# An attention and MLP layer in fp32: the place of one P V product, ScalarE's order of copies at two changes of weights, and the low halves of three weights in pieces

## The chip, the cores and the metric

One core of one Trainium2 chip. The metric is the device time of one execution of the whole program, in microseconds (us); lower is better. Three executions of the kernel before took 2776.44, 2777.89 and 2778.57 us. The names of the engines in the profile: PE (TensorE, matrix products), PEld (its weight loads), DVE (VectorE), ACT (ScalarE), POOL (GpSimd) and SP (SyncE, which issues the DMAs).

## The reference

Sixteen batches, each a 512 x 512 query x and a 512 x 512 context, go through one layer with 16 heads of 32:

```python
q = _layer_norm(query, ln1_g, ln1_b)
qh, kh, vh = q @ wq + bq, context @ wk + bk, context @ wv + bv
scores = einsum('bqhd,bkhd->bhqk', qh, kh) / sqrt(32)
scores = where(k <= q, scores, -inf)
o = einsum('bhqk,bkhd->bqhd', softmax(scores), vh)
x = query + o @ wo + bo
h = _layer_norm(x, ln2_g, ln2_b)
out = x + gelu(h @ w1 + b1) @ w2 + b2
```

w1 is 512 x 2048 and w2 is 2048 x 512. All is fp32.

## The kernel before

Dense products are made from two halves of each operand, a high half rounded to the short form fp32r and a low half, the rest: three matmuls (high x high, high x low, low x high) give one product. As a rule ScalarE writes a high half (a COPY or CAST) and VectorE the low half (a subtraction that waits for it).

**Preparation** (up to about 37 us). The four weights of attention are loaded; ScalarE writes their high halves and VectorE, in `weight_low` (L720), the low halves of wk, wv and wo, each with one instruction on 128 x 2048 elements. GpSimd at the same time splits the context of batch 0 into its halves, in `context` (L958): a CAST at L962 and a subtraction at L964 for each of four blocks. K's first product on TensorE (job K0) takes a block kt when `c_done` says so (L472).

**Stage A, attention** (to about 1424 us). Per batch there are 4 groups of 4 heads, and per group 12 steps; a step handles one tile of scores. Tiles k = 0 to 3 of a group (pair 0) hold the first two blocks of 128 queries of one head, tiles 4 to 11 (pair 1) one block each. Tile n = 12 g + k goes round like this: `score` (L500) on TensorE in step n; `mask_and_max` (L659) on VectorE; `exponential` (L852) on ScalarE; in groups 0 and 1 `scale` on GpSimd (L979); three steps later `p_transpose` (L515) on TensorE, into bank_t[n % 2]; in step n + 4 `move_tile` (L599) from that bank to pT, on ScalarE where `ACT_MOVES` names the tile and else on VectorE. When all tiles of a pair of a group are moved, `pv` (L528) multiplies them with V: pair 0 of group g in step 9 of that group, pair 1 in step 5 of the next. The buffers are narrow: `score` n waits for the mask of tile n - 2 (two banks), `p_transpose` n for the move of tile n - 2 (two banks), and a move of the next group's tile of a pair for that pair's `pv`.

Every engine runs the steps in the order of its own `body`. TensorE's (L576) is, in one step,

```python
score(it, n)
for job, i, j in steps:
    dense_step(it, job, g, i, j)
if k == PV1_AT and not (it.first and g == 0):
    pv(it, g - 1, 1)
if k == PV0_AT and not it.tail:
    pv(it, g, 0)
if n >= LAG and not it.tail or n < LAG and not it.first:
    p_transpose(it, n - LAG)
```

The dense jobs of table `BESIDE` fill the steps: in group 2, K3 in steps 2 and 3, V0b in 4 to 6, V1b in 7 to 9 and X0 to X3 (the transposes of the next batch's normalised x) in 7 to 10. For these VectorE computes the statistics and the normalisation (L627 to L640) in group 2's steps 1 and 4 to 7, ScalarE and VectorE the halves of the transposed x (`x_high` L825, `x_low` L643), and ScalarE copies V out (`v_copy`, L841) after the move of its step and ahead of the exponential. The first batch has no output products (jobs O and R), the last one no X jobs.

**Stage B, the MLP** (from about 1424 us) runs over the batches twice, once per half of the hidden units (phases 0 and 1). Its products use Strassen's scheme with 7 partial products. At the first batch of each phase (`first`) the halves of w2, and at the entry of part of w1, are still to be made: `w1_high` (L1689) and `w2_high` (L1707) on ScalarE, `w1_parts` and `w2_parts` (L1427, L1467) on VectorE, with sums (T1 to T4, S1 to S4) on VectorE between them. ScalarE's `body` (L1766) also copies the products P1, P5 and U2 of each half d out of TensorE's banks (`copy`, L1722): step (d, 3) of TensorE waits for P1's copy, (d, 4) for P5's and (d, 5) for U2's (L1319 to L1325). `a_high` (L1741) and VectorE's `a_low` make the halves of the activations for the second layer's products, `layer2` (L1338).

## Time and profile before

| what | value |
|---|---|
| median of 3 executions | 2777.89 us |
| the profiled execution's own time | 2778.07 us |
| its span, first to last instruction | 2776.2 us |
| mean granted clock of TensorE | 0.995 |
| PE, DVE, ACT, POOL busy | 98%, 74%, 60%, 32% of the span |
| one batch of attention (from one L687 of its group 2 to the next, 345.61 to 431.94) | 86.33 us |

The times in the rows count from the span's start. A row of the timeline has the start, the duration, the engine, the line, the operation with output and input, and how many instructions it merges; in brackets stands how long the engine had been idle, and who released it. Instructions of one engine overlap a little at their ends.

### The profile page before, as it was taken

Reading aid. Unit: us, or ns where it says so; the run is one execution under the profiler, and the core shown is the slowest. Engines: PE = TensorE matmul, PEld = TensorE weight load, DVE = VectorE, ACT = ScalarE, POOL = GpSimd, SP = SyncE. Lnnn points to the kernel's source line nnn. Section 1 sums busy time; section 2 is a strip of 40 time slices with the busy share of each in tenths; the row PEclk is TensorE's granted clock in tenths of the full one; section 3 lists DMA queues with packets and bytes.
Section 4 is the critical chain, followed back from the end, with each engine's and each line's share of the span. In section 5 each row is a group of like instructions: output and inputs, shape, how many; then the busy total and the mean of one; then the engine's idle time right before and its main releaser. Section 6 shows DMA issues by size and latency. Waiting matters only on the chain.

```text
span 2776.2 us, 67352 instructions
## 1 busy us (share of the span) xinstructions
PE 2730.1 (98%) x21928; PEld 2489.3 (90%) x21928; DVE 2041.0 (74%) x5205; ACT 1654.4 (60%) x4017; POOL 893.4 (32%) x842
## 2 busy tenths in 40 slices
PE   7999999999999999999979999999998999999999
PEld 6888888888888888888869999999998999999999
DVE  6777777777777777777698787787788566566556
ACT  5766667666676666766665656656556445444444
POOL 6657566575765656656510000000000000000000
PEclk9999999999999999999999999999999999999999
DMA  5233333333333323333243533534435433343342
GB/s 186 104 126 132 118 118 118 129 131 111 121 117 129 133 106 125 121 130 124 100 163 130 196 146 148 196 135 160 191 126 197 160 145 141 129 166 136 122 157 99
DMA packets 153084, 383.58 MB, mean 138 GB/s; under 512 B 13440, under 2 KB 17536, under 8 KB 144768
## 3 DMA queue, kind: packets, MB, share of 16 engines
q1 hardware_dynamic: 152960, 382.28, 37.1%
q14 instruction: 90, 0.74, 0.1%
q8 instruction: 34, 0.56, 0.1%
HBM read 172.51 MB, written 109.05 MB: 101 GB/s over the span
## 4 chain that ended last, share of the span: by engine, by line
PE 94%; DVE 2%; issue 2%; POOL 1%; ACT 1%; DMA 0%; SPq 0%; DVEq 0%; POOLq 0%; ACTq 0%
PE bank_d L495 19%; PE bank_t L525 11%; PE bank_s L1299 7%; PE bank_d L490 7%; PE bank_s L1300 6%; PE bank_s L1301 6%; PE bank_s L510 6%; PE bank_v L548 5%; PE bank_d L1299 5%; PE bank_d L1301 5%; PE bank_d L1300 5%; PE bank_v L1299 2%; PE bank_v L1300 2%; PE bank_v L1301 2%; PE bank_t L1299 1%
## 5 line engine op out<-in xcount | busy, mean ns | idle before, releaser
L862 ACT ACTIVATE sm<-sm,mins 128x128 f32<-128x128 f32 (+3 forms) x1024 | 572.0, 559 | 439.2 <-DVE mins L670 434.6
L989 POOL TENSOR_SCALAR sm<-sm,recips 128x128 f32<-128x128 f32 (+3 forms) x512 | 549.8, 1084 | 235.9 <-DVE recips L682 234.1
L670 DVE CUSTOM_DVE_ANT_0 sm<-bank_s,mask 128x128 f32<-128x128 f32 (+3 forms) x1024 | 474.3, 484 | 66.8 <-PE bank_s L510 64.0
L615 DVE COPY pT<-bank_t 128x384 f32<-128x384 f32 (+1 forms) x544 | 306.8, 564 | 210.6 <-PE bank_t L525 208.5
L1299 PE MATMUL bank_s<-w_hi,a_hi 128*128 128x256 f32 x1536 | 435.6, 284 | 2.1 <-DVE a_lo L1425 2.1
L1300 PE MATMUL bank_s<-w_lo,a_hi 128*128 128x256 f32 x1536 | 435.0, 283 | 0.0
L1301 PE MATMUL bank_s<-w_hi,a_lo 128*128 128x256 f32 x1536 | 434.9, 283 | 0.0
L525 PE MATMUL bank_t<-ident,sm 128*128 128x128 f32 x2560 | 412.8, 275 | 10.5 <-POOL sm L989 3.4
L525 PEld LDWEIGHTS bank_t<-ident,sm 128*128 128x128 f32 x2560 | 306.6, 140 | 92.3 <-issue 32.7
L1299 PE MATMUL bank_d<-b_hi,w_hi 128*128 128x256 f32 x1280 | 369.8, 289 | 14.0 <-ACT g L1726 7.7
L1301 PE MATMUL bank_d<-b_hi,w_lo 128*128 128x256 f32 x1280 | 364.3, 285 | 0.0
L1300 PE MATMUL bank_d<-b_lo,w_hi 128*128 128x256 f32 x1280 | 364.1, 284 | 0.0
L510 PE MATMUL bank_s<-stack 128*128 128x128 f32 (+3 forms) x1024 | 351.6, 384 | 0.0
L1299 PEld LDWEIGHTS bank_s<-w_hi,a_hi 128*128 128x128 f32 x1536 | 295.4, 192 | 3.1 <-DVE xr L1552 2.0
L1300 PEld LDWEIGHTS bank_s<-w_lo,a_hi 128*128 128x128 f32 x1536 | 295.3, 192 | 0.0
L1301 PEld LDWEIGHTS bank_s<-w_hi,a_lo 128*128 128x128 f32 x1536 | 295.2, 192 | 0.0
L1299 PEld LDWEIGHTS bank_d<-b_hi,w_hi 128*128 128x128 f32 x1280 | 247.5, 193 | 15.9 <-DVE w_lo L1425 14.2
L1506 DVE TENSOR_TENSOR g<-bank_d,g 128x512 f32<-128x512 f32 x160 | 110.4, 690 | 189.0 <-PE bank_d L1301 188.2
L1300 PEld LDWEIGHTS bank_d<-b_lo,w_hi 128*128 128x128 f32 x1280 | 247.8, 194 | 0.0
L1301 PEld LDWEIGHTS bank_d<-b_hi,w_lo 128*128 128x128 f32 x1280 | 247.5, 193 | 0.0
L1737 ACT ACTIVATE g<-g,vecb 128x256 f32<-128x256 f32 x384 | 174.7, 502 | 110.5 <-DVE g L1506 108.3
L1751 ACT CAST a_hi<-g 128x512 fp32r<-128x512 f32 x256 | 158.8, 621 | 113.6 <-PE bank_s L1301 110.9
(161 smaller groups left out, 6550.2 us busy)
## 6 DMA issues: line engine op xcount, KB each, us to landing
stack<-st_hi SPq DMA_DIRECT2D x256, 256.0 KB, 2.4
stack<-st_lo SPq DMA_DIRECT2D x128, 256.0 KB, 2.4
xr<-x_scratch SPq DMA_DIRECT2D x64, 512.0 KB, 4.2
b_scratch<-b_hi SPq DMA_DIRECT2D x16, 1792.0 KB, 9.1
b_scratch<-b_lo SPq DMA_DIRECT2D x16, 1792.0 KB, 12.8
b_hi<-b_scratch SPq DMA_DIRECT2D x16, 1792.0 KB, 7.3
b_lo<-b_scratch SPq DMA_DIRECT2D x16, 1792.0 KB, 11.2
xt<-in_x SPq DMA_DIRECT2D x64, 256.0 KB, 2.7
```

The lines of the kernel that those rows point to most:

```text
L490: mm = pe.matmul(out, left[part // 2][:, kt, cols], right[part % 2][:, kt, rows], start=(n == 0), stop=(n >= 18), skip_group_check=True)
L495: mm = pe.matmul(out, left[part // 2][:, kt, cols], right[part % 2][:, kt, rows], start=(at == 0), stop=(at == 11))
L510: mm = pe.matmul(bank_s[n % BANKS_S][:, off:off + w], stack[:, g % 2, 0, r, P * qt:P * qt + P], stack[:, g % 2, 1, r, 0:w], start=True, st ...
L525: mm = pe.transpose(bank_t[n % 2][:, P * c:P * c + P], sm[:, n % SLOTS_S, P * c:P * c + P], ident[:])
L615: copy(out, src).then_inc(moved[n % 2], 1)
L670: op = V.tensor_tensor_reduce(sm[:, n % SLOTS_S, off:off + w], bank_s[n % BANKS_S][:, off:off + w], mask[:, 512 - w:512], 1.0, 0.0, ALU.ad ...
L862: op = A.activation(row, row, ACT.Exp, bias=mins[:, g % 2, c:c + 1], scale=-1.0, accum_out=sums[:, g % 2, c:c + 1])
L989: op = G_.tensor_scalar(out=row, in0=row, scalar1=recips[:, g % 2, c:c + 1], scalar2=None, op0=ALU.mult)
L1299: pe.matmul(o, lh, rh, start=opens, stop=False, skip_group_check=True)
L1300: pe.matmul(o, lh, rl, start=False, stop=False, skip_group_check=True)
L1301: return pe.matmul(o, ll, rh, start=False, stop=True, skip_group_check=True)
L1737: op = A.activation(to, bank_x[d][:, C * m:C * m + C] if name == "C21" else to, ACT.Gelu, bias=vec[:, f:f + 1], scale=1.0)
```

## The change

1. In group 2, `pv` of group 1 runs in step 3, pair 0 and pair 1 one after the other, instead of pair 0 in group 1's step 9 and pair 1 in group 2's step 5. The other groups keep their places.
2. Of group 1's tiles ScalarE moves k = 3, 5 and 9 instead of 5, 9 and 11.
3. `weight_low` issues four subtractions of 128 x 512 instead of one of 128 x 2048; only the last one signals.
4. At the entry of stage B ScalarE makes S1 and S3 of w1 after the copy of P1 instead of before it.
5. At the first batch of each phase ScalarE copies P1, P5 and U2 of the half d = 1 ahead of most of the high halves of w2 that stood before them, and the activation high half (1, 0) comes after U2.

```diff
--- before.py
+++ after.py
@@ -41,7 +41,7 @@
     return 1, (k - 4) // 2, (2 + (k - 4) % 2,)
 
 
-ACT_MOVES = [(5, 9, 11), (5, 9, 11), (3, 5, 7, 9, 11), (5, 9, 11)]
+ACT_MOVES = [(5, 9, 11), (3, 5, 9), (3, 5, 7, 9, 11), (5, 9, 11)]
 
 
 def act_moves(n):
@@ -102,7 +102,7 @@
     TAIL = [("R", {5: 4}), ("O0", {7: 9, 8: 3}), ("O1", {7: 6, 9: 6}), ("O2", {10: 12}), ("O3", {11: 12})]
 
 
-    R_AT, PV1_AT, PV0_AT, O_PROD_AT, O_HIGH_AT, O_HIGH_LATE = 4, 5, 9, 6, 7, 11
+    R_AT, PV1_AT, PV0_AT, PV_AT, O_PROD_AT, O_HIGH_AT, O_HIGH_LATE = 4, 5, 9, 3, 6, 7, 11
 
     FEED_X_AT = 6
     STATS_AT, NORMALISE_AT = ((1, 8), (1, 11), (2, 1), (2, 4)), ((2, 5), (2, 6), (2, 6), (2, 7))
@@ -585,9 +585,13 @@
                         score(it, n)
                     for job, i, j in steps:
                         dense_step(it, job, g, i, j)
-                    if k == PV1_AT and not (it.first and g == 0):
+
+                    if k == PV_AT and g == 2:
+                        pv(it, g - 1, 0)
                         pv(it, g - 1, 1)
-                    if k == PV0_AT and not it.tail:
+                    if k == PV1_AT and g != 2 and not (it.first and g == 0):
+                        pv(it, g - 1, 1)
+                    if k == PV0_AT and g != 1 and not it.tail:
                         pv(it, g, 0)
                     if n >= LAG and not it.tail or n < LAG and not it.first:
                         p_transpose(it, n - LAG)
@@ -719,9 +723,10 @@
 
             def weight_low(i, done):
                 dve.wait_ge(w_hi_done, KT + i)
-                V.tensor_tensor(w_lo[i][:].rearrange("p t n -> p (t n)"), raw[i],
-                                w_hi[i][:].rearrange("p t n -> p (t n)").bitcast(F32),
-                                ALU.subtract).then_inc(done, 1)
+                for kt in range(KT):
+                    op = V.tensor_tensor(w_lo[i][:, kt, :], raw[i][:, D * kt:D * kt + D],
+                                         w_hi[i][:, kt, :].bitcast(F32), ALU.subtract)
+                op.then_inc(done, 1)
 
             for t in range(QT):
                 x_low(pro, f"X{t}", 0, 0)
@@ -942,8 +947,6 @@
                     if it.tail and n == 10:
                         feed_h_high("T4")
                         feed_w1_high(1, 1, ["A11", "A22", "A12"])
-                    if it.tail and n == 11:
-                        feed_w1_high(1, 1, ["S1", "S3"])
 
             over_batches(act, body)
             act.wait_ge(dense, tail_it.done("O3", 0))
@@ -1769,7 +1772,7 @@
             U = 4 * ph
             copy(c, 0, "P1")
             if first:
-                w1_high(U + 1, 1, ["S2"])
+                w1_high(U + 1, 1, ["S1", "S3", "S2"] if ph == 0 else ["S2"])
             copy(c, 0, "P5")
             if first:
                 w1_high(U + 1, 1, ["S4"])
@@ -1780,24 +1783,34 @@
             if first:
                 w2_high(U + 2, 0, ["B11", "B21", "B22"])
             activate(c, ph, 0, "C22")
+            copy(c, 1, "P1")
             if first:
-                w2_high(U + 2, 0, ["T1", "T3", "T2", "T4"])
-            copy(c, 1, "P1")
-            activate(c, ph, 0, "C21")
-            a_high(c, 1, 0)
-            if first:
-                w2_high(U + 3, 1, ["B11", "B21", "B22"])
-            copy(c, 1, "P5")
-            if norm:
-                x_high(c + 1, 0, x_bank(0))
-            if switch:
-                w1_high(4, 0, ["A11", "A22"])
-            activate(c, ph, 1, "C11")
-            if first:
-                w2_high(U + 3, 1, ["T1", "T3"])
-            if norm:
-                x_high(c + 1, 1, x_bank(1))
-            copy(c, 1, "U2")
+
+                w2_high(U + 2, 0, ["T1", "T3"])
+                activate(c, ph, 0, "C21")
+                copy(c, 1, "P5")
+                if norm:
+                    x_high(c + 1, 0, x_bank(0))
+                w2_high(U + 2, 0, ["T2", "T4"])
+                copy(c, 1, "U2")
+                a_high(c, 1, 0)
+                w2_high(U + 3, 1, ["B11", "B21", "B22", "T1"])
+                activate(c, ph, 1, "C11")
+                w2_high(U + 3, 1, ["T3"])
+                if norm:
+                    x_high(c + 1, 1, x_bank(1))
+            else:
+                activate(c, ph, 0, "C21")
+                a_high(c, 1, 0)
+                copy(c, 1, "P5")
+                if norm:
+                    x_high(c + 1, 0, x_bank(0))
+                if switch:
+                    w1_high(4, 0, ["A11", "A22"])
+                activate(c, ph, 1, "C11")
+                if norm:
+                    x_high(c + 1, 1, x_bank(1))
+                copy(c, 1, "U2")
             a_high(c, 0, 1)
             if norm:
                 x_high(c + 1, 2, x_bank(2))
```

The order of instructions at two places, as the program issues it. First TensorE at the start of group 2, from the end of step 3 (the last matmuls of K3) into step 4; L525 are the transposes of a tile, L510 scores, L490 the first matmuls of V0b, L548 is P V. Before:

```order
L495 MATMUL bank_d<-cT_hi,wk_lo 128x512
L525 MATMUL bank_t<-ident,sm 128x128 x3
L510 MATMUL bank_s<-stack 128x384
L490 MATMUL bank_d<-wv_hi,cT_hi 128x256
L490 MATMUL bank_d<-wv_lo,cT_hi 128x256
```

and with the change:

```order
L495 MATMUL bank_d<-cT_hi,wk_lo 128x512
L548 MATMUL bank_v<-pT,v_sb 32x256 x4
L548 MATMUL bank_v<-pT,v_sb 32x128 x4
L548 MATMUL bank_v<-pT,v_sb 32x256 x12
L548 MATMUL bank_v<-pT,v_sb 32x128 x4
L525 MATMUL bank_t<-ident,sm 128x128 x3
L510 MATMUL bank_s<-stack 128x384
L490 MATMUL bank_d<-wv_hi,cT_hi 128x256
```

Both blocks of P V now stand between K3 and the transposes of group 2's first tile (tile 24). In group 1, where pair 0 stood between the output product and the transposes of tile 18, it is gone.

Then ScalarE at the first batch of stage B, from the activation C22 of half 0 (L1737, with the change L1740) to the activations of half 1; L1705 (L1708) are high halves of w2, L1726 (L1729) the copies P1, P5 and U2 and L1751 (L1754) the activations' high halves, L1686 (L1689) the next batch's x. Before:

```order
L1737 ACTIVATE g<-g,vecb 128x256 x2
L1705 CAST w_hi<-s_sums 128x512 x2
L1705 CAST w_hi<-spare 128x512 x2
L1726 COPY g<-bank_d 128x2x256
L1737 ACTIVATE g<-bank_v,vecb 128x256 x2
L1751 CAST a_hi<-s_sums 128x512
L1705 CAST w_hi<-xr 128x512 x3
L1726 COPY g<-bank_d 128x2x256
L1686 ACTIVATE hT<-bank_t,vecb 128x512
L1737 ACTIVATE g<-g,vecb 128x256 x2
```

and with the change:

```order
L1740 ACTIVATE g<-g,vecb 128x256 x2
L1729 COPY g<-bank_d 128x2x256
L1708 CAST w_hi<-s_sums 128x512 x2
L1740 ACTIVATE g<-bank_v,vecb 128x256 x2
L1729 COPY g<-bank_d 128x2x256
L1689 ACTIVATE hT<-bank_t,vecb 128x512
L1708 CAST w_hi<-spare 128x512 x2
L1729 COPY g<-bank_d 128x2x256
L1754 CAST a_hi<-s_sums 128x512
L1708 CAST w_hi<-xr 128x512 x4
```

The first copy of a bank (P1) now comes before four high halves of w2 instead of after them, the second before the last two of these, and the third right behind them.

## Rows read from the trace of the kernel before

**Rows 1.** The page: the chain that ended last, by engine.

```profile
PE 94%; DVE 2%; issue 2%; POOL 1%; ACT 1%; DMA 0%; SPq 0%; DVEq 0%; POOLq 0%; ACTq 0%
```

**Rows 2.** Busy us of PE, PEld, DVE, ACT, POOL by stretch (stretch, its length, then busy).

```profile
340.00:354.00 14.00, 14.00 (x143) 12.45 (x142) 12.29 (x33) 9.27 (x23) 5.62 (x6) 1.00 0.20 76
1424.00:1471.00 47.00, 36.06 (x242) 34.38 (x241) 40.52 (x72) 32.20 (x61) 1.39 (x1) 0.82 0.33 128
2124.00:2153.00 29.00, 20.87 (x151) 19.91 (x150) 25.39 (x42) 18.73 (x38) 0.00 (x0) 0.88 0.32 111
```

**Rows 3.** Timeline of PE, batch 3, group 1 (start, us, engine, line, work).

```profile
318.37 1.72 PE L548 MATMUL bank_v<-pT,v_sb 128*32 128x256 f32 x32
...
327.18 0.39 PE L495 MATMUL bank_d<-wo_hi,oT_hi 128*128 128x512 f32 x1
327.40 0.40 PE L495 MATMUL bank_d<-wo_lo,oT_hi 128*128 128x512 f32 x1
327.73 0.86 PE L548 MATMUL bank_v<-pT,v_sb 128*32 128x256 f32 x16
328.52 0.55 PE L525 MATMUL bank_t<-ident,sm 128*128 128x128 f32 x3
328.82 0.42 PE L510 MATMUL bank_s<-stack 128*128 128x384 f32 x1
```

**Rows 4.** Timeline of PE, batch 3, group 2 and the start of 3.

```profile
339.37 0.49 PE L525 MATMUL bank_t<-ident,sm 128*128 128x128 f32 x3
...
354.07 0.49 PE L525 MATMUL bank_t<-ident,sm 128*128 128x128 f32 x3
354.32 0.47 PE L510 MATMUL bank_s<-stack 128*128 128x128 f32 x2
```

**Rows 5.** Timeline of DVE in the same stretch.

```profile
339.99 0.56 DVE L615 COPY pT<-bank_t 128x384 f32<-128x384 f32 x1 [0.97 <-PE bank_t L525]
...
344.67 0.56 DVE L615 COPY pT<-bank_t 128x384 f32<-128x384 f32 x1 [0.30 <-PE bank_t L525]
...
349.34 0.55 DVE L670 CUSTOM_DVE_ANT_0 sm<-bank_s,mask 128x384 f32<-128x384 f32 x1
...
352.57 0.69 DVE L648 TENSOR_TENSOR xnT_lo<-bank_d,xnT_hi 128x512 fp32r<-128x512 f32 x1 [0.76 <-ACT xnT_hi L828]
353.18 0.55 DVE L615 COPY pT<-bank_t 128x384 f32<-128x384 f32 x1
353.64 0.55 DVE L670 CUSTOM_DVE_ANT_0 sm<-bank_s,mask 128x384 f32<-128x384 f32 x1
```

**Rows 6.** Timeline of ACT in the same stretch.

```profile
349.89 0.59 ACT L828 CAST xnT_hi<-bank_d 128x512 fp32r<-128x512 f32 x1 [0.72 <-PE bank_d L438]
350.38 0.62 ACT L862 ACTIVATE sm<-sm,mins 128x384 f32<-128x384 f32 x1
...
351.94 0.60 ACT L828 CAST xnT_hi<-bank_d 128x512 fp32r<-128x512 f32 x1
```

**Rows 7.** Timeline of PE, batch 0, group 1.

```profile
70.80 0.66 PE L525 MATMUL bank_t<-ident,sm 128*128 128x128 f32 x4 [0.48 <-POOL sm L989]
```

**Rows 8.** Timelines of POOL, DVE and PE in the preparation.

```profile
14.47 1.59 POOL L962 CAST cT_hi<-c_raw 128x512 fp32r<-128x512 f32 x1 [2.15 <-DVE xt L640]
...
23.69 2.67 POOL L962 CAST cT_hi<-c_raw 128x512 fp32r<-128x512 f32 x1
...
14.19 1.41 DVE L708 SCALAR_TENSOR_TENSOR wq_lo<-pT,wq_scale,wq_hi 128x512 fp32r<-128x512 f32 x2
...
23.39 2.50 DVE L722 TENSOR_TENSOR wv_lo<-sm,wv_hi 128x2048 fp32r<-128x2048 f32 x1
...
27.75 0.50 PE L495 MATMUL bank_d<-cT_hi,wk_hi 128*128 128x512 f32 x1 [3.00 <-POOL cT_lo L964]
```

**Rows 9.** Timelines of PE at the entry and of DVE at the change of halves.

```profile
1443.57 0.66 PE L1291 MATMUL bank_t<-ident,xn 128*128 128x128 f32 x4 [1.93 <-DVE xn L1421]
...
2139.50 1.29 DVE L1425 TENSOR_TENSOR w_lo<-hT,w_hi 128x512 fp32r<-128x512 f32 x2 [1.48 <-ACT w_hi L1705]
```

## The prediction

> **What bounds the kernel now.** I read the page first: TensorE is busy 98% of the span, by its part on the engines, and makes 94% of the chain that ended last [rows 1]. So time goes only where TensorE loses an instruction's time, or gets a new wait. Then the busy time by stretch: in group 2 of a batch (steps 4 to 11) TensorE is busy 14.00 of 14.00 us, but VectorE 12.29 of them as well, with 1.7 us to spare; at the change of stages TensorE is busy 36.06 of 47.00 and VectorE 40.52, at the change of halves 20.87 of 29.00 and 25.39 [rows 2]. There TensorE waits, and VectorE is what it waits for in the long run. Last the timelines of one batch, read for who is how late; inner batches repeat with a period of 86.33 us.
>
> **Part 1, P V of group 1 in one block: the saving.** In group 1 the block of pair 0 starts 0.33 us after the last output matmul (327.40), and the transposes follow 0.79 later, at 328.52; output matmuls are 0.22 to 0.23 apart. The scores behind follow the transposes by 0.30 instead of 0.25 [rows 3, 4]. So the block costs 1.12 - 0.23 + 0.05 = 0.94 us. The block of pair 1 (x32 in the row, 1.72 us) is 0.86 longer than that of pair 0 (x16) for 512 more columns, 1.68 ns each [rows 3]. Pair 0's 384 columns thus need 0.645 us of work; the other 0.29 us is for getting into the small tiles and out of them. In one block with pair 1 it is paid once: TensorE saves 0.29 us a batch, 4.7 us over 16.
>
> **Part 1, what it makes late.** The block now stands ahead of the transposes of tile 24. TensorE gets there 0.94 us earlier than before, so the block starts at 339.37 - 0.94 + 0.10, and takes 0.65 + 1.65: the transposes go at 340.83 instead of 339.37 [rows 4], 1.46 later, though what follows V0b is 0.29 earlier. VectorE's copy of that tile, which waited for them at 339.99 [rows 5], is as late. VectorE has no gap from there to its wait at 344.67, 0.30 us long, 0.40 with the 0.1 by which two instructions may overlap. So from 344.67 on VectorE is 1.46 - 0.40 = 1.06 us late, where TensorE is 0.29 early. The two engines stood still in step with each other before; now VectorE runs behind.
>
> Up to step 8 the buffers hold it. I followed scores and transposes one by one: the mask of tile 29 is done some 0.2 us before its scores' bank is wanted, the normalised x of X0 0.1 us before. Then ScalarE, whose exponentials wait for the masks, runs without the gap of 0.72 us that it had at 349.89 [rows 6]. It takes the delay on: the mask of tile 32 at 349.34 [rows 5] becomes 350.40, the exponential behind it 350.98 instead of 350.38, and the CAST of X2 (third in line) 352.54 instead of 351.94 [rows 6]. VectorE's low half follows 0.63 behind that CAST (352.57 before), then the copy of tile 30 at 353.78 instead of 353.18, done at 354.33 [rows 5]. The transposes of tile 32 need its bank. They went at 354.07 [rows 4], and would go at 353.78: they **wait to 354.35, 0.56 us**. The next scores, due 0.25 later, need the mask of tile 34, which moves from 353.64 to 354.24 and is done at 354.87: another 0.30. Sum 0.86 lost, 0.29 saved: **0.57 us slower per batch**. VectorE is level again with TensorE two steps later, so nothing goes on into group 3. Fourteen inner batches: +8.0 us.
>
> Batch 0: its group 1 has no output products, and TensorE waits there for GpSimd's scaling just behind the place the block is taken from (0.48 us at 70.80 [rows 7]), so the 0.94 us earlier is mostly not had: 0.57 + 0.94 = +1.5. The last batch has no X jobs and no statistics: VectorE catches up, -0.3. **Part 1 in all: +9.2 us.** Bounds per inner batch: -0.29 (nothing binds) and +1.2 (0.86 lost and, of 1.06, the rest too, with nothing saved).
>
> **Part 2, ScalarE's moves.** A COPY of some 0.6 us goes from VectorE to ScalarE at step 19 of a batch and back at step 27. At step 27 VectorE stood idle 0.97 us before 339.99 [rows 5], which covers it, and the block waits for this copy no longer than for K3 to end. Nothing gained, nothing lost. Without that cover the block itself would start up to 0.6 late.
>
> **Part 3, the low halves in pieces.** Only the last piece signals, so what can change is GpSimd. Its CAST at 14.47 took 1.59 us and the one at 23.69 took 2.67, ending both times 0.47 us after VectorE's subtractions of two operands in SBUF [rows 8]. TensorE waited 3.00 us for the block behind the second. In the first case VectorE ran two pieces one behind the other (x2, 14.19 to 15.60), and GpSimd did not get in between them. I take that row: no entry at a seam. Then pieces only add their seams. The nearest bound is 1.41 us for two pieces of 512, so at most 2.8 for four against 2.5 [rows 8]; less here, where a plain subtraction of 512 lets the next start after 0.61 (352.57 to 353.18 [rows 5]). I take 0.2 for each of wk and wv, both on the way to GpSimd's last block: **+0.4 us**. The other bound is the whole wait gone, -3.0. wo's pieces end before the first mask is due.
>
> The Trainium skill, "SBUF — State Buffer", section "Who interferes with whom", says that VectorE with two SBUF inputs and GpSimd reading SBUF exclude each other for a whole instruction, and that the second to issue is blocked until the first finishes. By that rule each seam would let GpSimd in, after 0.6 us instead of 2.3, and the sum would have -3.0 in place of +0.4. The row at 14.47 speaks against it.
>
> **Parts 4 and 5, the order of copies.** At the entry P1's copy comes 2 us earlier, but TensorE then meets its wait for the normalised x at 1443.57 [rows 9], which hangs on VectorE's unbroken work ahead of it: nothing is left of it. After it, TensorE's steps (1, 3) to (1, 5) no longer wait for ScalarE's copies, which are most of the 8.1 us that it is idle at the change of halves [rows 2]. It runs up to 8 us ahead, and then waits in `layer2` for VectorE's a_low (0, 1), and again for (1, 1) and (2, 0). VectorE had only 3.6 us without work in those 29 us, and 6.5 of 47 at the entry [rows 2]. The longest of these gaps, 1.48 us before the low half of T1 at 2139.50 [rows 9], closes, since T1's high half now comes ahead of an activation; about 0.5 opens elsewhere, as T1 and T2 of w2's first part come behind a copy of 0.6. **-1.0 at the change of halves, -0.9 at the entry**, which has the same queue and the next batch's x in it. Bounds: 0, and the gaps whole, -3.6 and -6.5.
>
> **Sum** against the profiled execution's 2778.07 us (span 2776.2): 9.2 + 0.4 - 1.9 = +7.7, so 2785.8. The median of the runs is 0.2 lower than that execution: **2785.6 us**.
>
> **The rivals.**
> 1. *The seams let GpSimd in*, part 1 as above. TensorE's K0 ends 3.0 us earlier. For it: GpSimd waits there for nothing else, its loads having landed. Against: the row at 14.47. 2785.6 - 3.4 = 2782.2 us. By the skill's rule this is the case. Chance 0.25.
> 2. *VectorE's lateness does not reach TensorE* (the other side, faster). The place is the transposes of tile 32. Before, tile 30's copy ended at 353.73, 0.34 us ahead of them [rows 4, 5]; if VectorE and ScalarE make good all but 0.05 us of the delay by then, 0.29 us a batch is kept: -4.7 + 0.4 - 1.9, 2771.7 us, and 2768.3 with rival 1. For it: 1.7 us of slack in 14 [rows 2]. Against: the gaps are mostly waits for ScalarE, which is late itself. Chance 0.22.
> 3. *The lateness costs at V's and X's banks too*: X3 takes V1b's bank, which ScalarE's copy frees; by my count it is free 0.04 us in time. If ScalarE is 0.5 later there, each batch loses 0.5 more: +7, 2793 us. Chance 0.08.
>
> My forecast has 0.45; its own range is 2783 to 2789 (0.2 us either way per batch, and half of the last part). **Range** 2769 to 2789: it leaves out rival 3 and the tail of rival 2. A measurement of this kernel tells 0.2% (5.6 us) from no change: faster is below 2772.3, slower above 2783.4. Faster: rival 2 but for its edge, 0.2. Same: rival 1 and edges, 0.29. Slower: 0.51.
>
> **What would show it.** Part 1: blocks of x48 rows on L548 in group 2, one batch 86.9 us instead of 86.33, and TensorE waiting about 0.5 us for VectorE's pT before the transposes at the end of group 2, in each inner batch; VectorE idle near 3 us ahead of tile 24's copy. If those waits are missing, rival 2 holds. Part 3: GpSimd's CASTs beside wk's and wv's low halves still above 2 us; at 0.6 to 1.2, rival 1. Parts 4 and 5: the waits for ScalarE's g gone, one wait of some 5 us for a_lo in their place. I am wrong if the period stays below 86.33, or if the two changes give over 3 us each.

## The result and the profile after

The changed kernel takes 2784.1 us in the median of 11 runs (2782.58 to 2785.43), the kernel before, run beside it, 2776.36 (11 runs, 2774.25 to 2778.57). The ratio is 1.0028, with a 95% interval of 1.0021 to 1.0036: slower, by 7.7 us. The time and its cause in attention came as forecast. Two smaller terms had the wrong sign, and the errors nearly cancelled.

The profiled execution of the changed kernel has a span of 2783.0 us, 6.8 more than the one before. To see where that lies I take marks that are in both programs: VectorE's COPYs out of the P V bank, two in each batch (one in group 1, one in group 2), and its sums out of bank_t in stage B. In the timeline of VectorE before (start, us, engine, line, work) they are these; the first row is the first COPY of batch 0, the second and third are the second COPYs of batches 3 and 4, the fourth is the last COPY of attention:

```profile
65.95 0.67 DVE L687 COPY rT<-bank_v 128x512 f32<-128x512 f32 x1
...
345.61 0.69 DVE L687 COPY rT<-bank_v 128x512 f32<-128x512 f32 x1
...
431.94 0.68 DVE L687 COPY rT<-bank_v 128x512 f32<-128x512 f32 x1
...
1381.84 0.68 DVE L687 COPY rT<-bank_v 128x512 f32<-128x512 f32 x1
...
1483.54 0.70 DVE L1552 TENSOR_TENSOR xr<-bank_t,xr 128x512 f32<-128x512 f32 x1
...
2115.19 0.70 DVE L1552 TENSOR_TENSOR xr<-bank_t,xr 128x512 f32<-128x512 f32 x1
...
2163.54 0.68 DVE L1552 TENSOR_TENSOR xr<-bank_t,xr 128x512 f32<-128x512 f32 x1
```

And after:

```profile
63.09 0.67 DVE L691 COPY rT<-bank_v 128x512 f32<-128x512 f32 x1
...
346.35 0.68 DVE L691 COPY rT<-bank_v 128x512 f32<-128x512 f32 x1
...
433.31 0.68 DVE L691 COPY rT<-bank_v 128x512 f32<-128x512 f32 x1
...
1389.38 0.69 DVE L691 COPY rT<-bank_v 128x512 f32<-128x512 f32 x1
...
1491.52 0.68 DVE L1555 TENSOR_TENSOR xr<-bank_t,xr 128x512 f32<-128x512 f32 x1
...
2123.17 0.68 DVE L1555 TENSOR_TENSOR xr<-bank_t,xr 128x512 f32<-128x512 f32 x1
...
2170.39 0.68 DVE L1555 TENSOR_TENSOR xr<-bank_t,xr 128x512 f32<-128x512 f32 x1
```

The differences between neighbours give the ledger of the 6.8 us:

| stretch | before, us | after, us | difference | forecast |
|---|---|---|---|---|
| start to the first P V copy (the preparation) | 65.95 | 63.09 | -2.86 | +0.4 |
| first to last P V copy (attention) | 1315.89 | 1326.29 | +10.40 | +9.2 |
| to the first sum out of bank_t (entry of stage B) | 101.70 | 102.14 | +0.44 | -0.9 |
| across the change of halves | 48.35 | 47.22 | -1.13 | -1.0 |

From batch 1 on, the P V copies of neighbouring batches stand 86.32 us apart before, in most batches, and 86.96 after. The ledger compares one execution of each kernel.

**Attention.** In the timeline of TensorE the place of the block and the place of the wait look like this (start, us, engine, line, work, and in brackets the idle time and what ended it):

```profile
338.14 2.37 PE L548 MATMUL bank_v<-pT,v_sb 128*32 128x256 f32 x48
340.44 0.55 PE L525 MATMUL bank_t<-ident,sm 128*128 128x128 f32 x3
...
352.94 0.60 PE L525 MATMUL bank_t<-ident,sm 128*128 128x128 f32 x4
353.30 0.48 PE L510 MATMUL bank_s<-stack 128*128 128x512 f32 x1
354.15 0.52 PE L525 MATMUL bank_t<-ident,sm 128*128 128x128 f32 x3 [0.37 <-DVE pT L619]
354.53 0.50 PE L510 MATMUL bank_s<-stack 128*128 128x128 f32 x2
```

The block is one of x48. The transposes of tile 32 answer to those at 354.07 [rows 4], and they wait for VectorE's copy of pT. The bracket gives 0.37 us, but they start 0.85 us behind the scores ahead of them (353.30), where the kernel before has 0.32, counted from this row of its timeline of TensorE:

```profile
353.75 0.48 PE L510 MATMUL bank_s<-stack 128*128 128x512 f32 x1
```

So 0.53 us are lost at this place, and another 0.13 at the scores behind (0.38 us behind their transposes instead of 0.25). Over the whole program this kind of wait went from 2.5 us in 4 places to 8.0 us in 19 (the waits of TensorE, after: line waited for, us in total, times, longest):

```profile
PE bank_t L525 <- DVE pT L619: 8.0, 19, 1.3
```

VectorE itself, in the same stretch, has a hole behind the block and then none until a wait for ScalarE at 352.85:

```profile
341.12 0.56 DVE L619 COPY pT<-bank_t 128x384 f32<-128x384 f32 x1 [3.11 <-PE bank_t L525]
...
345.41 0.55 DVE L619 COPY pT<-bank_t 128x384 f32<-128x384 f32 x1
...
352.85 0.69 DVE L652 TENSOR_TENSOR xnT_lo<-bank_d,xnT_hi 128x512 fp32r<-128x512 f32 x1 [1.01 <-ACT xnT_hi L833]
353.46 0.55 DVE L619 COPY pT<-bank_t 128x384 f32<-128x384 f32 x1
```

The COPY at 345.41 is the one that had waited 0.30 us at 344.67 [rows 5]: the gap is gone, as the forecast had it.

**Preparation.** GpSimd's CASTs of the context answer to those at 14.47 and 23.69 [rows 8]:

```profile
14.39 0.94 POOL L965 CAST cT_hi<-c_raw 128x512 fp32r<-128x512 f32 x1 [2.15 <-DVE xt L644]
...
19.88 0.81 POOL L965 CAST cT_hi<-c_raw 128x512 fp32r<-128x512 f32 x1 [0.95 <-DMA c_raw<-in_ctxT]
...
22.30 1.07 POOL L965 CAST cT_hi<-c_raw 128x512 fp32r<-128x512 f32 x1
```

The fourth CAST, 2.67 us before, now takes 1.07, and it runs beside wk's pieces instead of wv's low half. The price is on VectorE and shows in TensorE's wait, now for wk's low half instead of for GpSimd (first VectorE, then TensorE):

```profile
18.92 3.97 DVE L727 TENSOR_TENSOR wk_lo<-pT,wk_hi 128x512 fp32r<-128x512 f32 x4
...
22.95 0.50 PE L495 MATMUL bank_d<-cT_hi,wk_hi 128*128 128x512 f32 x1 [1.78 <-DVE wk_lo L727]
```

**Stage B.** At the entry and at the change of halves TensorE waits once for a long time for VectorE's a_low (timeline of TensorE):

```profile
1441.21 0.55 PE L1302 MATMUL bank_d<-b_hi,w_hi 128*128 128x256 f32 x1 [2.84 <-ACT g L1729]
...
1452.67 0.66 PE L1294 MATMUL bank_t<-ident,xn 128*128 128x128 f32 x4 [1.42 <-DVE xn L1424]
...
1468.26 0.55 PE L1302 MATMUL bank_s<-w_hi,a_hi 128*128 128x256 f32 x1 [6.14 <-DVE a_lo L1428]
...
2149.00 0.56 PE L1302 MATMUL bank_s<-w_hi,a_hi 128*128 128x256 f32 x1 [5.13 <-DVE a_lo L1428]
```

The transposes at 1452.67 answer to 1443.57 [rows 9]: 9.1 us later. The program is 7.5 us late at the start of this stretch, so 1.6 are lost between.

### The profile page after: what moved, and what is told of

It reads as the page before. It is cut to its first block, busy times and chain, and to the rows that moved or that the text cites. A ratio compares the mean times of both kernels' runs of the same rounds, so it can differ in the third digit from the quotient of the medians.

```text
span 2783.0 us, 67361 instructions
## 1 busy us (share of the span) xinstructions
PE 2731.0 (98%) x21928; PEld 2488.2 (89%) x21928; DVE 2039.8 (73%) x5214; ACT 1652.3 (59%) x4017; POOL 890.5 (32%) x842
## 4 chain that ended last, share of the span: by engine, by line
PE 48%; DVE 2%; issue 1%; ACT 1%; POOL 0%; DMA 0%; DVEq 0%; ACTq 0%; POOLq 0%
PE bank_s L1302 6%; PE bank_s L1303 6%; PE bank_s L1304 6%; PE bank_d L1302 5%; PE bank_d L1304 5%; PE bank_d L1303 5%; PE bank_v L1302 2%; PE bank_v L1303 2%; PE bank_v L1304 2%; PE bank_d L495 1%; PE bank_t L1302 1%; PE bank_t L1304 1%; PE bank_t L1303 1%; PE bank_t L525 1%; PE bank_t L1294 1%
## 5 line engine op out<-in xcount | busy, mean ns | idle before, releaser
L525 PE MATMUL bank_t<-ident,sm 128*128 128x128 f32 x2560 | 412.5, 275 | 16.8 <-DVE pT L619 8.0
L525 PEld LDWEIGHTS bank_t<-ident,sm 128*128 128x128 f32 x2560 | 305.9, 140 | 98.7 <-issue 29.7
L510 PE MATMUL bank_s<-stack 128*128 128x128 f32 (+3 forms) x1024 | 351.8, 384 | 0.0
L1740 ACT ACTIVATE g<-g,vecb 128x256 f32<-128x256 f32 x384 | 174.6, 502 | 108.6 <-DVE g L1509 106.6
L1754 ACT CAST a_hi<-g 128x512 fp32r<-128x512 f32 x256 | 158.7, 621 | 113.6 <-PE bank_s L1304 110.8
```

Source lines behind the costliest of these rows:

```text
L510: mm = pe.matmul(bank_s[n % BANKS_S][:, off:off + w], stack[:, g % 2, 0, r, P * qt:P * qt + P], stack[:, g % 2, 1, r, 0:w], start=True, st ...
L525: mm = pe.transpose(bank_t[n % 2][:, P * c:P * c + P], sm[:, n % SLOTS_S, P * c:P * c + P], ident[:])
L1740: op = A.activation(to, bank_x[d][:, C * m:C * m + C] if name == "C21" else to, ACT.Gelu, bias=vec[:, f:f + 1], scale=1.0)
L1754: A.copy(a_part(a_hi, k, h), a_source(k, h)).then_inc(a_hi_ok, 1)
```

## The experiments

Each kernel is told as a change of the kernel before or of the changed one, with its five readings in the table at the end of this section.

**pieces** has part 3 alone.

> The kernel before with nothing but the low halves of wk, wv and wo in four pieces each. Theory: the whole 2.9 us by which the first copy out of the P V bank came earlier in the changed kernel (65.95 to 63.09 us) comes from this part, since GpSimd gets into the seams between pieces; the run is then 2.9 us under the kernel before (ratio 0.9990), with that copy near 63.1. Rival, what my prediction held: GpSimd gets no seam and the pieces cost 0.4 us; the 2.9 came from elsewhere (another state of the entry), and the copy is near 66.3.

**pv_moves** has parts 1 and 2 alone, **pv_only** part 1 without the new list of moves:

```
-ACT_MOVES = [(5, 9, 11), (3, 5, 9), (3, 5, 7, 9, 11), (5, 9, 11)]
+ACT_MOVES = [(5, 9, 11), (5, 9, 11), (3, 5, 7, 9, 11), (5, 9, 11)]
```

> The kernel before with nothing but both P V blocks of group 1 in step 3 of group 2 and the list of ScalarE's copies of group 1. Theory: it carries all of the loss of attention, 10.4 us (ratio 1.0037), 0.63 us in each middle batch (period 86.33 to 86.96 us). Rival: part of the loss of a batch is made by the other parts (through SBUF state or code loading), and this run stays under 8 us.

> As pv_moves, but with ScalarE's copies of pT in group 1 at tiles 5, 9 and 11 as before. Theory: the list of copies is worth nothing beside the block (prediction: 0), so this run is within 0.1 us per batch of pv_moves, 9 to 12 us over the kernel before. Rival: the block is what costs and the new list gives part of it back, since it takes the copy of tile 23 off ScalarE where the x copies queue; then this run is 2 us or more slower than pv_moves.

**after_stats** is the changed kernel with one number changed:

```
-    STATS_AT, NORMALISE_AT = ((1, 8), (1, 11), (2, 1), (2, 4)), ...
+    STATS_AT, NORMALISE_AT = ((1, 8), (1, 11), (2, 1), (2, 3)), ...
```

> The changed kernel with the fourth row statistic of the next batch (statistics of tile 3, the aggregates and the sum with epsilon, 1.2 us of VectorE's time) one step earlier, in step 3 of group 2, where VectorE idles 3.1 us behind the P V block. Theory: TensorE's loss of a batch is VectorE's lateness behind that hole (waits of 0.37 us for the copy of pT at tile 32 and more for scores), so filling the hole takes it away: the period falls from 86.96 to about 86.0 (the saving of one entry into tile mode then stands alone, 0.3 under the period of before), the time to about 2770. Rival: the loss is in TensorE itself (a block of two P V lengths with nothing beside it, or tile mode entered at a worse place); then the period stays at 86.9 and the time at 2784.

Measured, beside a kernel before of 2777.47 us (21 runs): pieces 2774.68 us, ratio 0.9994 (0.9985 to 1.0003); pv_moves 2788.22, 1.0035 (1.0021 to 1.0049); pv_only 2785.56, 1.0036 (1.0022 to 1.0049); after_stats 2769.38, **0.9974 (0.9965 to 0.9983)**, faster than both kernels.

The block alone carries the loss in attention: the period is 86.97 us in pv_moves and in pv_only, so the list of moves is worth nothing there. (pv_only is 8.1 us over the kernel before, a little under the 9 to 12 expected; with 5 runs each the medians of the two kernels don't tell them apart.) The statistic decides between the two theories on part 1. VectorE now does it in the hole (timeline of VectorE, after_stats):

```profile
334.68 0.69 DVE L631 BATCH_NORM_STATS2 stats<-xt 128x6 f32<-128x512 f32 x1
335.28 0.41 DVE L637 BATCH_NORM_AGGREGATE mv<-stats 128x2 f32<-128x6 f32 x4
...
337.87 0.56 DVE L619 COPY pT<-bank_t 128x384 f32<-128x384 f32 x1 [1.97 <-PE bank_t L525]
```

and TensorE goes through the end of the group without a wait (timeline of TensorE, after_stats; the third and fourth row answer to 354.15 and 354.53 above):

```profile
349.46 0.60 PE L525 MATMUL bank_t<-ident,sm 128*128 128x128 f32 x4
349.81 0.48 PE L510 MATMUL bank_s<-stack 128*128 128x512 f32 x1
350.13 0.49 PE L525 MATMUL bank_t<-ident,sm 128*128 128x128 f32 x3
350.38 0.47 PE L510 MATMUL bank_s<-stack 128*128 128x128 f32 x2
```

The period is 86.03, 0.29 under the 86.32 of before: the saving that I had read out of the two block lengths. (The runs show it for one block less; that it is the way into and out of the small tiles is the reading, and no run separates it.) The loss of a batch was VectorE's lateness, and it was 86.96 - 86.03 = 0.93 us.

A reading of pieces against the others was not what I expected. The first P V copy is at 63.90 us, 2.05 earlier than before, but in pv_only, which has no pieces at all, it is at 62.27. So the early start isn't the pieces' alone. That made the next experiments compare the preparation too.

**before_stats** is the control: the same number changed in the kernel before.

> Control for after_stats: the kernel before with the same statistic one step earlier and nothing else. Theory: in the kernel before VectorE has no hole in that step and TensorE does not wait for it at tile 32, so moving 1.2 us of VectorE's work is worth nothing: period 86.32 us as before, time within 1 us of the kernel before. Rival: the statistic's place is what limits either kernel and the gain has nothing to do with the P V block; then the period falls by 0.3 us or more here too, to 2772 or less.

**entry_b** has part 4 alone, **halves** part 5 alone, and **after_stats_s13** is after_stats with part 4 taken back:

```
+                    if it.tail and n == 11:
+                        feed_w1_high(1, 1, ["S1", "S3"])
...
-                w1_high(U + 1, 1, ["S1", "S3", "S2"] if ph == 0 else ["S2"])
+                w1_high(U + 1, 1, ["S2"])
```

> The kernel before with nothing but the copies of S1 and S3 of the second half moved behind the copy of P1 at the entry of stage B. Stretch measured: from the last copy out of the P V bank of attention's last group to the first sum out of bank_t, 101.70 us before. Theory: the order of ScalarE gives 0.9 us (100.8), as in the changed kernel with the statistics moved (100.76), and the 102.14 of the changed kernel has 1.4 us of TensorE at half clock on top, which does not belong to the edit. Rival: the edit itself brings the half clock (TensorE waits 2.8 us for a copy just there) and costs 0.4 (102.1). The time is within 1 us of the kernel before by either; the stretch decides.

> The kernel before with nothing but the copies P1, P5 and U2 of half 1 ahead of the high halves of w2, in the first batch of each phase. Stretch measured: between the sums out of bank_t on either side of the change of halves, 48.35 us before, 47.22 in the changed kernel. Theory: the gain of 1.1 us there is this part's alone: 47.2, and nothing elsewhere (first stretch 101.7 by this part, and more only if its edit in the first batch of phase 0 acts there). Rival: it needs the other edit of ScalarE's order; then 48.3. Time about 2776, 1 us under the kernel before.

> The changed kernel with the statistic moved as in after_stats, and S1 and S3 back where they stood before, in attention's last step. Theory: part 4 is worth 0.9 us, so this run is 0.9 us slower than after_stats (stretch 101.7 instead of 100.8). Rival: part 4 costs 0.4 by the half clock and this run is that much faster. The period of attention stays 86.03 us in both.

Measured beside 2777.44 us (33 runs): before_stats 2775.46, ratio 0.9998 (0.9989 to 1.0007); entry_b 2778.18, 1.0004 (0.9995 to 1.0013); halves 2772.57, 0.9991 (0.9982 to 1.0000); after_stats_s13 2769.49, 0.9979 (0.9970 to 0.9988). Only the last is clear of no change; for the others the stretches decide. (halves is 4.9 us under the kernel before, where its two stretches give 2.1.)

The control keeps its period, 86.32 to 86.33: the statistic's place is worth nothing without the block, so the hole and its filling belong together. (Its median is 2.0 us under that of the kernel before, but the interval includes no change; both kernels' runs lie in two groups, as told below.) For stage B the theory that I took into these runs fell. The 1.0 us at the entry comes with part 5 (halves: 101.70 to 100.70 us), whose code runs in the first batch of phase 0 too, and the 1.1 at the change of halves as well (47.24). Part 4 gives nothing: 102.06 with it alone, and 100.76 against 100.65 with and without it beside part 5. 102.06 is the number of the rival, but not for its reason: in the 12 us from 50 us behind the last P V copy, where the rival put the lower clock, entry_b's granted clock is 1.00. TensorE's long wait for a_lo is part 5's doing, with all else as before (timeline of TensorE, halves):

```profile
2136.06 0.55 PE L1299 MATMUL bank_s<-w_hi,a_hi 128*128 128x256 f32 x1 [5.14 <-DVE a_lo L1425]
```

The other 1.4 us of the changed kernel's entry, in this execution, are its clock. Over the same 8 us of the program, the stretch of 8.00 us from 54 us behind the last P V copy, the busy time of PE, PEld, DVE, ACT and POOL, the granted clock, the DMA share and GB/s were in the changed kernel

```profile
1443.38:1451.38 8.00, 7.87 (x52) 7.67 (x51) 5.58 (x15) 5.27 (x11) 1.40 (x1) 0.76 0.74 316
```

in after_stats

```profile
1428.68:1436.68 8.00, 5.74 (x46) 5.37 (x46) 7.06 (x18) 5.28 (x12) 1.40 (x1) 1.00 0.74 316
```

and in pv_moves, which has the old order of ScalarE's copies,

```profile
1446.76:1454.76 8.00, 7.81 (x52) 7.61 (x51) 5.58 (x15) 4.80 (x10) 1.40 (x1) 0.77 0.74 316
```

At a mean of 0.76 TensorE ran part of these 8 us at the lower of its levels, 1.2 GHz. Its matmuls of 128x256 start 0.21 us apart there instead of 0.12 in after_stats, and VectorE, which waits for it, was busy 1.5 us less. pv_only has a clock of 1.00 in that stretch, and its entry takes 101.80 against pv_moves' 103.25. But the fall itself is there too, in the 4 us just ahead (pv_only):

```profile
1438.25:1442.25 4.00, 3.80 (x21) 3.54 (x20) 3.65 (x6) 3.40 (x5) 0.00 (x0) 0.57 0.75 314
```

In the same 4 us the kernel before has 0.64 and halves 0.57; after_stats and entry_b have 1.00. So the clock falls there in kernels with the old order and with the new, about where TensorE waits (in the changed kernel 2.84 us up to 1441.21). In halves the fall cost nothing: its entry takes 100.70 us, that of after_stats, without it, 100.76. In the changed kernel and in pv_moves it lasted on into the matmuls, and cost 1.4 us. The edit does not decide which. What does so stays open: after_stats waits 2.9 us at the same place with no fall at all.

**before_wait** tests the preparation. Of the kernels with whole low halves, pv_only, entry_b, halves and before_stats had the first P V copy at 61.9 to 62.3 us, before and pv_moves at 65.95 and 65.32. One wait is added in the kernel before, ahead of wv's low half:

```
+            dve.wait_ge(c_done, KT)
             weight_low(2, w_lo_done)
```

**best_wait** joins parts 1, 2 and 5, the moved statistic and this wait, without pieces and without part 4. **best_g3** goes on from there:

```
-                    if k == PV_AT and g == 2:
+                    if k == PV_AT and g in (2, 3):
```

(and the two old places left out for these groups).

> The kernel before with one wait more on VectorE in the preparation: the whole low half of wv starts only when GpSimd has done its fourth low half of the context. Theory: the executions of the kernel before fall into two groups 3 us apart (2774.5 and 2777.6) by which engine issues first at about 23.4 us, VectorE its subtraction of 2.5 us or GpSimd its CAST; with the wait GpSimd always does, the CAST takes 0.61 instead of 2.67 us, the first copy out of the P V bank is at 62.0 to 62.5 us, and all runs lie within 1 us of 2774.5. Rival: the two groups have another cause, and the runs stay spread over 4 us, or the wait makes wv's low half late for V0a and all lie above 2776.

> Part 1 and 2 and part 5 of the change, the statistic moved as in after_stats, whole low halves with the wait of before_wait, S1 and S3 where they stood before. Theory: the terms add: preparation as before_wait (copy at 62.0 to 62.5), period 86.03, entry of stage B 100.7, change of halves 47.2: 2768.0 us, about 9 under the kernel before and 1 to 1.5 under after_stats. Rival: the pieces were worth as much as the wait; then 2769.4, as after_stats.

> best_wait with P V of group 2 also in one block, in step 3 of group 3. Theory: each block less saves TensorE one entry into the small tiles and one way out, 0.29 us, where VectorE's hole behind the block does no harm; group 3 has no x to normalise, so the period falls to 85.74 and the time by 4.6 us to 2763.5. Rival: VectorE or GpSimd (its scaled copies stop after group 1, but its expansion of the reciprocals falls there) is late behind the new hole and TensorE waits as it did in group 2; then the period stays at 86.0 to 86.6 and the time at 2768 or above.

Measured beside 2777.49 us (18 runs): before_wait 2775.05, ratio 0.9994 (0.9985 to 1.0003); best_wait 2769.32, **0.9975 (0.9965 to 0.9986)**; best_g3 2793.56, 1.0061 (1.0048 to 1.0075).

The 18 runs of the kernel before fall into two groups, 8 at 2774.12 to 2775.13 us and 10 at 2777.46 to 2778.23, with nothing between; in the 54 of the two comparisons before this one, 13 do lie between, though none from 2776.11 to 2777.20. With the wait 9 of 11 are at 2774.43 to 2775.42, and the other two at 2776.46 and 2776.81, which the expectation did not have and nothing here explains. The interval of before_wait includes no change.

The profile of before_wait can't test the wait. GpSimd's fourth CAST, 2.67 us at 23.69 in the kernel before [rows 8], takes 0.61 in it, but 0.61 as well in pv_only, entry_b, halves and before_stats, which have no wait. What separates these from before and pv_moves lies further up. TensorE's matmuls of Q0 are slower in them (timeline of TensorE, first before, then before_stats):

```profile
19.40 0.39 PE L495 MATMUL bank_d<-xnT_hi,wq_hi 128*128 128x512 f32 x1
```

```profile
19.48 0.63 PE L495 MATMUL bank_d<-xnT_hi,wq_hi 128*128 128x512 f32 x1
```

They start 0.43 us apart instead of 0.23. So ScalarE's high half of Q0 comes at 23.06 instead of 21.93, VectorE's low half of Q0 behind it comes later too, and VectorE reaches wv's subtraction at 24.5 instead of 23.39, when GpSimd is past its CAST. Where Q0 is fast, VectorE is at wv 0.30 us ahead of the CAST and GpSimd is shut out for 2.5 us. All six profiled kernels with whole low halves and no wait are of one kind or the other: slow Q0, CAST 0.61 and a first P V copy at 61.9 to 62.3 us, or fast Q0, CAST 2.67 and 65.3 to 66.0. The durations of the slow Q0 are those that such matmuls have at the lower clock (0.63 us in pv_moves' batch 0, below), but the profile shows no lower clock there, so that cause is argued, not shown.

The wait is tested by best_wait, which has the fast Q0 (0.39). VectorE stands ready and waits (timelines of GpSimd and of VectorE, best_wait):

```profile
23.39 0.62 POOL L966 CAST cT_hi<-c_raw 128x512 fp32r<-128x512 f32 x1
...
25.39 2.29 DVE L725 TENSOR_TENSOR wv_lo<-sm,wv_hi 128x2048 fp32r<-128x2048 f32 x1 [2.19 <-POOL cT_lo L968]
```

The CAST takes 0.62, and the first P V copy is at 62.21. best_g3, with the same wait and a fast Q0, has 62.18. That the two groups of times are these two outcomes fits every profiled execution, but no trace of the kernel before from the lower group was kept.

best_wait came out 1.3 us above its expectation and level with after_stats: its stretches are those expected (62.21, 86.03, 100.60 and 47.23 us), and its profiled span of 2766.7 us is only 0.5 under that of after_stats. The pieces are worth about as much as the wait, as the rival had it. Where the missing 1.3 us of the median went is not shown.

best_g3 was wrong by 30 us and in sign: the period is 87.4 to 87.7, above the rival's 86.0 to 86.6 too. The rival's mechanism is what its profile shows. VectorE has a second hole, behind the block of group 3, and TensorE's waits for pT are up from 2.5 us in 4 places (best_wait) to 10.0 in 27 (timeline of VectorE, then waits of TensorE, best_g3):

```profile
365.68 0.56 DVE L618 COPY pT<-bank_t 128x384 f32<-128x384 f32 x1 [3.43 <-PE bank_t L525]
```

```profile
PE bank_t L525 <- DVE pT L618: 10.0, 27, 1.3
```

and the wait at the end of group 2 is back as well, since VectorE doesn't catch up in a batch (timeline of TensorE, batch 3):

```profile
354.43 0.52 PE L525 MATMUL bank_t<-ident,sm 128*128 128x128 f32 x3 [0.37 <-DVE pT L618]
...
368.02 0.49 PE L525 MATMUL bank_t<-ident,sm 128*128 128x128 f32 x3
368.49 0.50 PE L510 MATMUL bank_s<-stack 128*128 128x512 f32 x1
```

(The scores at 368.49 stand 0.47 behind their transposes instead of 0.25, with no wait named: many of such small delays carry no bracket.) The waits that the profile names are 7.5 us more, of some 22 us lost in attention against best_wait, and no run fills the second hole: that all of the loss is VectorE's lateness is read from the profile here, not shown.

The readings of all, from the marks of the first section:

| kernel | first P V copy | batch 0 | period | entry of B | halves | median |
|---|---|---|---|---|---|---|
| before | 65.95 | 82.73 | 86.32 | 101.70 | 48.35 | 2776.36 |
| changed | 63.09 | 84.20 | 86.96 | 102.14 | 47.22 | 2784.1 |
| pieces | 63.90 | 82.71 | 86.32 | 101.72 | 48.34 | 2774.68 |
| pv_moves | 65.32 | 85.78 | 86.97 | 103.25 | 48.35 | 2788.22 |
| pv_only | 62.27 | 84.25 | 86.97 | 101.80 | 48.35 | 2785.56 |
| after_stats | 62.57 | 83.33 | 86.03 | 100.76 | 47.26 | 2769.38 |
| before_stats | 61.93 | 82.73 | 86.33 | 101.75 | 48.33 | 2775.46 |
| entry_b | 62.09 | 82.75 | 86.32 | 102.06 | 48.34 | 2778.18 |
| halves | 61.89 | 82.75 | 86.32 | 100.70 | 47.24 | 2772.57 |
| after_stats_s13 | 63.37 | 84.23 | 86.03 | 100.65 | 47.23 | 2769.49 |
| before_wait | 62.18 | 82.73 | 86.33 | 101.88 | 48.32 | 2775.05 |
| best_wait | 62.21 | 83.34 | 86.03 | 100.60 | 47.23 | 2769.32 |
| best_g3 | 62.18 | 84.97 | 87.4 to 87.7 | 102.45 | 47.22 | 2793.56 |

(Batch 0 is the distance from its first P V copy to the first of batch 1. The first five readings are of one profiled execution each, the last is the median of all. The kernel before had 2776.36 beside the changed one and 2777.44 to 2777.49 beside the others. best_g3's entry loses its 1.9 us against best_wait in its first 22 us, still in the last group of attention.)

Two values of batch 0 stand out: pv_moves' 85.78 against pv_only's 84.25, and after_stats_s13's 84.23 against the 83.33 of after_stats. Both are the clock (5 us of pv_moves, with the columns as above; pv_only has 1.00 in them):

```profile
70.00:75.00 5.00, 4.54 (x17) 3.63 (x18) 3.32 (x14) 3.04 (x10) 4.99 (x5) 0.66 0.01 3
```

All of the 1.5 us are lost over these matmuls, which take 0.63 us instead of 0.39. after_stats_s13 has 0.72 from 66 to 72 us, where the others of its kind have 1.00, and loses its 0.9 there.

## Why the prediction was right, and where it was not

**The time.** 2785.6 us was forecast with a range of 2769 to 2789, 2784.1 was measured; +7.7 us of change in both. That closeness is partly luck, as the parts show: the two profiled executions are 6.8 us apart, and errors of up to 3.3 us cancelled.

**Part 1, right in mechanism and nearly in size.** "0.86 lost, 0.29 saved" per batch: the runs give 0.93 lost and 0.29 saved, 0.64 net instead of 0.57. The saving was shown by taking the lateness away (period 86.03), the loss by the difference. The place was right (tile 32's transposes wait for the copy of tile 30), and so was the size there: they go 0.53 us later behind the scores ahead of them, where 0.56 was forecast (the 0.37 in the bracket is only the part of it in which TensorE stood idle). The division behind it was off: the next scores lose 0.13, not 0.30, and some 0.2 are lost ahead, where I had the buffers hold: 0.07 at X0's transposes (at 345.55; VectorE's normalisation ends at 345.49), 0.07 at X3's, and 0.05 behind each. "Batch 0 +1.5" was 84.20 - 82.73 = 1.47. "The last batch -0.3": from the copy of batch 15 to the last one of attention it is 23.71 us instead of 23.99. The fourteen batches between gave 9.2 us of difference instead of 8.0. Rival 2, that VectorE's lateness does not reach TensorE, was false, but it names the version worth having: after_stats is that case, at 2769.4 us where the rival with the seams had 2768.3.

**Part 2, right: nothing.** pv_only and pv_moves have the same period. pv_moves' profiled execution lost 1.5 us more in batch 0, but that was a fall of the clock (0.66 from 70 to 75 us), and the changed kernel, which has the list, doesn't show it.

**Part 3, wrong.** The step that failed is "I take that row: no entry at a seam". In the kernels with pieces the third and fourth CAST, both beside wk's pieces now, take 0.65 to 1.13 us, so GpSimd does get in. The row at 14.47, 1.59 us, on which I argued, has two values: 1.59 or 1.60 us in before, pv_moves, pv_only and after_stats, and 0.93 or 0.94 in the nine others, with the code of that stretch the same in all. VectorE's two pieces take 1.41 us together in the four and 1.76 in the nine, where the CAST got in between. I had one sample of two outcomes and read it as a rule. The rule of the Trainium skill that I set against it ("SBUF — State Buffer", "Who interferes with whom") was the better guide at these seams: by it the sum would have had -3.0, and the trace has -2.86. But pieces are not the only way to the gain: before_wait reaches 62.18 us without pieces, earlier than any kernel with them (62.57 to 63.90), and best_wait reaches 62.21 with VectorE ready ahead of GpSimd. wk's pieces, with GpSimd in between, take 3.97 us instead of 2.28 in the changed kernel, and TensorE waits 1.78 for them. What the pieces buy is that the bad outcome at 23.4 us no longer happens; against the good one they lose 0.3 to 2.0 us. Rival 1 therefore held, though its 3.0 us is right only against the execution that was profiled.

**Parts 4 and 5, half right.** "One wait of some 5 us for a_lo" in place of the waits for ScalarE is there (5.13), and the two terms are -1.1 and -1.0 where -1.0 and -0.9 were forecast. Both belong to part 5, as the experiments show. That nothing is left of part 4 was forecast; measured it is between +0.1 and +0.4. The entry of the changed kernel nevertheless took 0.44 more, not 0.9 less, for 1.4 us of lower clock that no step of mine had. That is this one execution's; the profiles kept don't say how many of the others had it.

So the sum's +7.7 stands on +10.4 where I had +9.2, -2.9 where I had +0.4, and +0.4 where I had -0.9: errors of +1.2, -3.3 and +1.3 that cancelled to -0.8, with -0.1 from the change of halves. Beyond them, the median of the kernel before mixes two groups 3 us apart, and its profile is of the slower one; a forecast from one profile can't see that.

## What to carry over

Work that is gathered into one block on the busiest engine makes a hole on the engine that feeds it, and that engine is late behind the hole, not during it; find a job without inputs from the block (here 1.2 us of row statistics) and put it into the hole in the same edit, or the saving is paid back three times over (0.93 lost against 0.29 saved). Before a rule is built on one row of a trace, look at the same row in other executions: it may be one of two outcomes. Then follow it upstream, since what decides it can lie on a third engine (here 1.1 us more or less of TensorE's first product), and a wait that fixes the order can be worth as much as a faster operation. An edit of order in a queue should be tested in every place where its code runs: the gain at the entry came from the part that was made for the change of halves.

## What the runs showed of the hardware

VectorE's subtraction of two SBUF operands and GpSimd's CAST and subtraction exclude each other, in both directions. The CAST took 2.67 us when it came behind VectorE's 2.5 us subtraction, and 0.61 or 0.62 when it came ahead of it. wv's whole subtraction took 2.29 us when it started after GpSimd was done (best_wait) and 2.92 when it started 0.5 us into GpSimd's last one (timeline of VectorE, before_stats):

```profile
24.52 2.92 DVE L722 TENSOR_TENSOR wv_lo<-sm,wv_hi 128x2048 fp32r<-128x2048 f32 x1
```

In four pieces it took 3.60 us beside the same work of GpSimd (the changed kernel, at 23.48).

TensorE's granted clock in the same 8 us of the same work was 1.00 in some kernels and 0.76 in others, at a cost of 1.4 us. It had fallen in the 4 us ahead in most of them, while TensorE waited, and came back sooner or later. pv_moves and pv_only, which differ only in which engine copies two tiles of each batch, are on either side; why is open.
